# Rebuilding the attention of layer 1: two sets of head buffers, exponentials by pairs of heads, normalisation of three batches by DMA, products on GpSimd, and a new order on every engine

## The reference

```python
x = x + _L1_attn_ref(_L1_cond_ref(x, side, side, L1_cond_w, L1_cond_u, cond), ..., Wqkv, Wproj, bproj)
# attention: 16 heads of 16, no mask
attn = softmax(einsum('gqd,gkd->gqk', q, k) / sqrt(16));  ctx = einsum('gqk,gkd->gqd', attn, v)
out = ctx @ Wproj.T + bproj
# a gate: a, b decay by `decay` at each token, forward and backward
ek = exp(min(k, 30)); ekv = ek * v;  nf, df = scan(ekv, ek);  nb, db = reverse scan(ekv, ek)
euk = exp(min(u + k, 30))
num = nf + nb - ekv + euk * v;  den = df + db - ek + euk
out = sigmoid(r) * (num / max(den, 1e-8)) * (0.8 + 0.2 * tf)
```

## Time and profile before

| | |
|---|---|
| median of 3 runs | 1052.66 us (1048.91 to 1054.09) |
| span of the profiled execution | 1051.6 us |
| PE busy | 919.1 us (87%) |
| DVE busy | 787.0 us (75%) |
| ACT busy | 522.8 us (50%) |
| POOL busy | 248.1 us (24%) |
| attention of layer 1 | about 413 to 595 us of the span |

### The profile page before, as it was taken

How to read it: one execution, slowest core, us unless ns; L and a number is a source line. 1 busy time by engine, 2 the same in 40 slices (tenths; PEclk the granted TensorE clock), 3 DMA queues, 4 the chain that set the end, 5 groups by cost and what they waited for, 6 DMA issues and landing times.

```text
span 1051.6 us, 14776 instructions
## 1 busy us (share of the span) xinstructions
PE 919.1 (87%) x5524; PEld 674.8 (64%) x5524; DVE 787.0 (75%) x1188; ACT 522.8 (50%) x781; POOL 248.1 (24%) x288
## 2 busy tenths in 40 slices
PE   2899896999999998798888989995868886999998
PEld 1566665777777886555555868862446664778886
DVE  7898883559999895778767689888849897554444
ACT  6354455345545544356366444436747667243332
POOL 5122213023334241000020022301513224012221
PEclk9999998999999999899889999998889999899999
DMA  6000000243434331000000233224010000133331
GB/s 248 1 2 2 1 1 1 100 133 96 145 111 146 113 115 38 1 1 1 1 1 1 71 120 117 91 77 104 1 60 1 1 1 2 30 112 109 117 106 60
DMA packets 28518, 64.07 MB, mean 61 GB/s; under 512 B 10240, under 2 KB 12032, under 8 KB 27680
## 3 DMA queue, kind: packets, MB, share of 16 engines
q1 hardware_dynamic: 28448, 63.14, 18.5%
HBM read 60.37 MB, written 2.76 MB: 60 GB/s over the span
## 4 chain that ended last, share of the span: by engine, by line
PE 58%; DVE 21%; ACT 11%; issue 7%; POOL 1%; DMA 1%; DVEq 0%; SPq 0%; ACTq 0%; POOLq 0%
PE bank L1749 11%; PE bank L1750 10%; PE bank L1751 10%; PE bank L647 4%; PE bank L673 3%; ACT probs L794 2%; DVE act_lo L2098 2%; PE bank L756 2%; DVE wkv_y L192 2%; DVE bank L2093 1%; PE bank L705 1%; DVE bank L2084 1%; PE bank L2327 1%; DVE wkv_y L269 1%; DVE act_s L920 1%
## 5 line engine op out<-in xcount | busy, mean ns | idle before, releaser
L1749 PE MATMUL bank<-h_hi,w_gu_hi 128*128 128x512 f32 x416 | 168.1, 404 | 14.9 <-DVE act_lo L2098 9.9
L1896 ACT ACTIVATE act_s<-bank 128x512 f32<-128x512 f32 x104 | 62.0, 597 | 222.0 <-PE bank L1751 222.0
L1750 PE MATMUL bank<-h_hi,w_gu_lo 128*128 128x512 f32 x416 | 165.7, 398 | 0.0
L1751 PE MATMUL bank<-h_lo,w_gu_hi 128*128 128x512 f32 x416 | 165.5, 398 | 0.0
L2084 DVE TENSOR_TENSOR bank<-bank,c_rows 128x512 f32<-128x512 f32 x94 | 65.1, 692 | 87.9 <-PE bank L1751 87.9
L2015 POOL TENSOR_TENSOR w_d_lo<-w_raw,w_d_hi 128x256 fp32r<-128x256 f32 x52 | 46.8, 900 | 266.7 <-ACT w_d_hi L1890 266.7
L1749 PEld LDWEIGHTS bank<-h_hi,w_gu_hi 128*128 128x128 f32 x416 | 78.8, 189 | 40.8 <-issue 18.6
L794 ACT ACTIVATE probs<-bank 128x1536 f32<-128x1536 f32 (+1 forms) x32 | 53.0, 1657 | 95.8 <-PE bank L705 87.6
L1751 PEld LDWEIGHTS bank<-h_lo,w_gu_hi 128*128 128x128 f32 x416 | 79.0, 190 | 19.5
L2010 POOL TENSOR_TENSOR w_gu_lo<-w_raw,w_gu_hi 128x512 fp32r<-128x512 f32 x52 | 71.6, 1377 | 80.1 <-ACT w_gu_hi L1885 80.1
L1750 PEld LDWEIGHTS bank<-h_hi,w_gu_lo 128*128 128x128 f32 x416 | 79.0, 190 | 17.3
(11 more groups left out here) (346 smaller groups left out, 1813.3 us busy)
## 6 DMA issues: line engine op xcount, KB each, us to landing
w_raw<-in_L_w SPq DMA_DIRECT2D x52, 384.0 KB, 3.1
c_rows<-c_L SPq DMA_DIRECT2D x26, 512.0 KB, 3.7
c_rows<-c_L SPq DMA_DIRECT2D x6, 448.0 KB, 3.7
w_attn<-in_L_w_attn SPq DMA_DIRECT2D x2, 1280.0 KB, 7.6
c_rows<-c_L SPq DMA_DIRECT2D x6, 384.0 KB, 3.5
c_rows<-c_L SPq DMA_DIRECT2D x6, 320.0 KB, 3.5
c_rows<-c_L SPq DMA_DIRECT2D x6, 256.0 KB, 3.9
lora_chunks<-w_raw SPq DMA_DIRECT2D x4, 384.0 KB, 2.6
```

Of the source, the lines that this page charges most:

```text
L1749: pe.matmul(o, w_hi, r_hi, start=start, stop=False)
L1750: pe.matmul(o, w_lo, r_hi, start=False, stop=False)
L1751: return pe.matmul(o, w_hi, r_lo, start=False, stop=stop)
L1896: act.activation(act_s[:, half, :], bank[2 * half][:, :], ACT.Silu).then_inc(self.silu, 1)
```

## The change

- **Buffers.** Queries and keys, and the values, get a second set (`heads_2`, `values_2`), which lie over buffers of the experts that are idle in this stage; batches alternate. The maxima get space for all four groups. Scores alternate between banks 0, 1 and banks 2, 3, so step p waits for the maxima of step p-2.
- **Exponentials by pairs.** The transposed scores use banks 4 and 5 only, two heads at a time: `scores_t_pe(b, g, i)` with 4 matmuls in two row groups, then `exp_act(b, g, i)` on 128 x 1024, then the other pair.
- **Normalisation by DMA.** For batches 0 to 2, `sums_pe`, `inv_dve`, `spread_pe` and `norm_dve` are gone. SP writes the four rows of sums to DRAM, reads them back as 128 x 32, DVE takes the reciprocals of that tile, SP writes them to DRAM and broadcasts them to 128 x 1024, and GpSimd multiplies `work[:, b]`. Batch 3 is normalised as before.
- **Gate units.** GpSimd makes the product of the exponential with the side input (two instructions), the sum, and the product with the reciprocal; DVE keeps `den`, one Newton step and the last product.
- **Transposes** of the maxima are ordinary matmuls against an identity, both operands in tiles of the type float32r.
- **Order.** All four functions are written anew; projections of batch b+1 stand between the steps of batch b. The splits of the first weights of `F1` move from the end of batch 2 to the end of batch 3 on ACT, and behind all gate work on GpSimd.

```diff
+heads_2 = under("heads_2", [P, 2 * GROUPS, T])
+values_2 = under("values_2", [P, 2, N])
+sums_2 = under("sums_2", [P, 2, 512])
+sums_dram = nc.dram_tensor("head_sums", (B - 1, 4, N), F32).ap()
+inv_dram = nc.dram_tensor("head_inverses", (B - 1, 4, N), F32).ap()
...
+def pooled_den_dve(dve, o):
+    dve.wait_ge(wkv_exp, o + 1)
+    dve.wait_ge(wkv_bwd, 2 * o + 2)
+    dve.scalar_tensor_tensor(out=wkv_y[:, :, 1, :], in0=wkv_e[:, :, :], scalar=E30, in1=wkv_y[:, :, 1, :],
+                             op0=ALU.min, op1=ALU.add).then_inc(wkv_den, 1)
+def newton_dve(dve, o):
+    den = wkv_y[:, :, 1, :]
+    dve.wait_ge(wkv_ln, 2 * by_ln(o))
+    dve.scalar_tensor_tensor(out=den, in0=den, scalar=1e-8, in1=wkv_e[:, :, :], op0=ALU.add, op1=ALU.mult).then_inc(wkv_inv, 1)
+def pooled_out_dve(dve, o):
+    n, b = UNITS[o]
+    dve.wait_ge(wkv_inv, inv_at(o) + 2)
+    dve.wait_ge(wkv_summed, pool_steps(o) + 2)
+    dve.scalar_tensor_tensor(out=G[:, G_SLOT[n], :, b * T:b * T + T], in0=wkv_y[:, :, 1, :], scalar=2.0,
+                             in1=wkv_num[:, :, :], op0=ALU.subtract, op1=ALU.mult).then_inc(g_done, 1)
+def ev_pool(pool, o):
+    b = UNITS[o][1]
+    pool.wait_ge(wkv_exp, o + 1)
+    pool.wait_ge(g_done, o)
+    pool.tensor_scalar(wkv_num[:, :, :], wkv_e[:, :, :], E30, -1.0, ALU.min, ALU.mult).then_inc(wkv_ev, 1)
+    pool.wait_ge(wkv_ev, pool_steps(o) + 1)
+    pool.tensor_tensor(wkv_num[:, :, :], wkv_num[:, :, :], side[:, :, b * T:b * T + T], ALU.mult).then_inc(wkv_ev, 1)
+def pooled_sum_pool(pool, o):
+    pool.wait_ge(wkv_ev, pool_steps(o) + 2)
+    pool.wait_ge(wkv_bwd, 2 * o + 2)
+    pool.tensor_tensor(wkv_num[:, :, :], wkv_num[:, :, :], wkv_y[:, :, 0, :], ALU.subtract).then_inc(wkv_summed, 1)
+def product_pool(pool, o):
+    pool.wait_ge(wkv_ln, 2 * by_ln(o))
+    pool.wait_ge(wkv_summed, pool_steps(o) + 1)
+    pool.tensor_tensor(wkv_num[:, :, :], wkv_num[:, :, :], wkv_e[:, :, :], ALU.mult).then_inc(wkv_summed, 1)
...
+    self.qk = (qk, heads_2)
+    self.v = (v_sb, values_2[:, 0, :].rearrange("p (t c) -> p t c", t=2))
+    self.inverse = (values_2[:, 1, :], act_s[:, :, :].rearrange("p a t -> p (a t)"))
+    self.maxes = act_hi[:, :, :].rearrange("p a (g h c) -> p (a g) h c", g=2, h=2)
+    self.ident = act_lo[:, 0, 0:P]
+    self.sums = sums_2[:, 1, 0:32]
+    self.inverses = sums_2[:, 1, 32:64]
+    self.tanh = prob_mem[:, 2 * N:4 * N].rearrange("p (k t) -> p k t", k=KC)
...
+def score_banks(self, p):
+    return 2 * (p % 2)
+def scores_pe(self, pe, b, p):
+    f, m = self.first + b, self.qk[b % 2]
+    if p in (0, 4):
+        pe.wait_ge(n_copied, 4 * f + p // 2 + 2)
+    if b or p >= 2:
+        pe.wait_ge(n_maxed, 8 * f + p - 1)
...
+def scores_t_pe(self, pe, b, g, i):
+    m = self.qk[b % 2]
+    pe.wait_ge(n_added, 4 * (self.first + b) + g + 1)
+    if b or g or i:
+        pe.wait_ge(n_exp, self.half_group(b, g, i) - 1)
+    for k, q0, at in self.keys:
+        for j in (2 * i, 2 * i + 1):
+            rows = slice(SLOT * j, SLOT * j + SLOT)
+            mm = pe.matmul(bank[4 + j % 2][:, at:at + T], m[rows, GROUPS + g, k * P:k * P + P],
+                           m[rows, g, 0:T], start=True, stop=True, tile_position=(SLOT * j, 0))
+    mm.then_inc(n_scores_t, 1)
...
+    if sources[-1] < B - 1:
+        pe.wait_ge(n_scaled, sources[-1] + 1)
+    if sources[0] == 0:
+        if tb == 0:
+            pe.wait_ge(n_maxed, 8 * (self.first + B))
+        if tb == 2:
+            pe.wait_ge(n_exp, self.half_group(B - 1, 3, 1))
...
 def pe(self, pe):
     pe.wait_ge(attn_w[self.name], 32)
+    for b in range(-1, B + 1):
+        self.scores_t_pe(pe, b, 0, 0)
+        self.mix_pe(pe, b - 1, 3)
+        self.scores_pe(pe, b, 5)
         self.turn_pe(pe, b, 1)
         self.scores_pe(pe, b, 6)
+        self.scores_t_pe(pe, b, 0, 1)
+        self.proj_pe(pe, b + 1, 0)
+        self.scores_t_pe(pe, b, 1, 0)
         self.mix_pe(pe, b, 0)
         self.turn_pe(pe, b, 2)
         self.scores_pe(pe, b, 7)
+        self.scores_t_pe(pe, b, 1, 1)
+        self.proj_pe(pe, b + 1, 1)
+        self.scores_t_pe(pe, b, 2, 0)
+        self.mix_pe(pe, b, 1)
         self.turn_pe(pe, b, 3)
+        self.scores_t_pe(pe, b, 2, 1)
+        self.scores_pe(pe, b + 1, 0)
+        self.proj_pe(pe, b + 1, 2)
+        self.scores_pe(pe, b + 1, 1)
+        self.scores_t_pe(pe, b, 3, 0)
+        self.proj_pe(pe, b + 1, 3)
+        self.scores_pe(pe, b + 1, 2)
+        self.scores_t_pe(pe, b, 3, 1)
+        self.mix_pe(pe, b, 2)
+        if b == B - 1:
+            self.out_pe(pe, 0, range(B - 2))
+        self.turn_pe(pe, b + 1, 0)
+        self.scores_pe(pe, b + 1, 3)
+        self.scores_pe(pe, b + 1, 4)
+        self.values_pe(pe, b + 1)
+    self.out_pe(pe, 1, range(B - 2))
     self.sums_pe(pe, B - 1)
+    self.out_pe(pe, 0, (2,))
+    self.out_pe(pe, 1, (2,))
     self.spread_pe(pe, B - 1, 0)
     self.spread_pe(pe, B - 1, 1)
     self.out_pe(pe, 0, (B - 1,))
...
     self.out_pe(pe, 2, range(B))
     self.out_pe(pe, 3, range(B))
...
+def exp_act(self, act, b, g, i):
+    at = self.half_group(b, g, i)
+    act.wait_ge(n_scores_t, at)
+    if b or g >= 2:
+        act.wait_ge(n_mixed, 4 * (self.first + b) + g - 1)
+    elif g == 1:
+        act.wait_ge(n_gated, self.first + B)
+    act.activation(self.p_t[g % 2][:, 2 * i:2 * i + 2, :], banks[:, 4:6, :], ACT.Exp).then_inc(n_exp, 1)
...
 def act(self, act):
     self.tanh_act(act)
+    for b in range(-1, B + 1):
+        self.exp_act(act, b - 1, 3, 0)
         self.heads_act(act, b, 3)
+        self.relu_act(act, b, 0)
+        self.ln_act(act, b, 0)
+        self.row_act(act, b, 1)
+        self.exp_act(act, b - 1, 3, 1)
+        self.exp_act(act, b, 0, 0)
+        self.ctx_act(act, b - 1, 1)
         self.scale_act(act, b, 1, 0)
+        self.scale_act(act, b, 1, 1)
+        self.exp_act(act, b, 0, 1)
+        self.units_exp_act(act, b, 1)
+        self.heads_act(act, b + 1, 0)
+        self.exp_act(act, b, 1, 0)
+        self.relu_act(act, b, 1)
+        self.ln_act(act, b, 1)
+        self.exp_act(act, b, 1, 1)
+        self.row_act(act, b + 1, 0)
+        self.heads_act(act, b + 1, 1)
+        self.exp_act(act, b, 2, 0)
         self.ctx_act(act, b, 0)
+        self.scale_act(act, b + 1, 0, 0)
+        self.exp_act(act, b, 2, 1)
+        self.scale_act(act, b + 1, 0, 1)
+        self.heads_act(act, b + 1, 2)
+        self.units_exp_act(act, b + 1, 0)
+        if b == B - 1:
             for p in (0, 1):
                 F1.split_gu_act(act, p)
                 F1.split_d_act(act, p)
...
+def inverse_dve(self, dve, b):
+    dve.wait_ge(n_norm_in, 160 * b + 80)
+    dve.reciprocal(self.inverses, self.sums).then_inc(n_inv, 1)
 def dve(self, dve):
+    for b in range(1, B):
+        self.gate_dve(dve, b)
+    for b in range(B + 1):
+        self.inverse_dve(dve, b - 2)
+        self.newton_dve(dve, b - 1, 1)
+        self.max_dve(dve, b - 1, 7)
+        self.made_dve(dve, b - 1, 1)
+        self.scan_dve(dve, b, 0, False, 0)
+        self.add_dve(dve, b - 1, 3)
+        self.scan_dve(dve, b, 0, False, 1)
+        self.scan_dve(dve, b, 0, True, 0)
+        self.scan_dve(dve, b, 0, True, 1)
         self.max_dve(dve, b, 0)
+        self.den_dve(dve, b, 0)
         self.max_dve(dve, b, 1)
         self.max_dve(dve, b, 2)
         self.add_dve(dve, b, 0)
+        self.newton_dve(dve, b, 0)
         self.max_dve(dve, b, 3)
+        self.max_dve(dve, b, 4)
+        self.made_dve(dve, b, 0)
         self.values_dve(dve, b)
+        self.scan_dve(dve, b, 1, False, 0)
+        self.scan_dve(dve, b, 1, False, 1)
         self.add_dve(dve, b, 1)
+        self.scan_dve(dve, b, 1, True, 0)
+        self.scan_dve(dve, b, 1, True, 1)
         self.max_dve(dve, b, 5)
+        self.den_dve(dve, b, 1)
         self.max_dve(dve, b, 6)
         self.add_dve(dve, b, 2)
...
+def scaled_pool(self, pool, b):
+    pool.wait_ge(n_norm_in, 160 * b + 160)
+    m = work[:, b, :]
+    pool.tensor_tensor(m, m, self.inverse[b % 2], ALU.mult).then_inc(n_scaled, 1)
...
+def pool(self, pool):
+    ones = self.v[1]
+    ends = sum_rows[:, :, :].rearrange("p g c -> p (g c)")
+    pool.wait_ge(self.x_ready, self.x_value)
+    pool.tensor_tensor(act_hi[:, 0, :], ends, ends, ALU.subtract).then_inc(n_zeroed, 1)
+    pool.wait_ge(self.x_ready, self.x_value + 2)
+    pool.tensor_tensor(act_hi[:, 1, :], ends, ends, ALU.subtract).then_inc(n_zeroed, 1)
+    pool.tensor_copy(self.ident, ident[:, :]).then_inc(n_zeroed, 1)
+    pool.memset(ones, 0.0).then_inc(n_zeroed, 1)
+    pool.wait_ge(n_zeroed, 5)
+    pool.memset(ones[:, :, 16::SLOT], 1.0).then_inc(n_zeroed, 1)
+    for b in range(B + 1):
+        self.ev_pool(pool, b, 0)
+        self.sum_pool(pool, b, 0)
+        self.product_pool(pool, b, 0)
+        self.scaled_pool(pool, b - 2)
+        self.ev_pool(pool, b, 1)
+        self.sum_pool(pool, b, 1)
+        self.product_pool(pool, b, 1)
+    for p in (0, 1):
+        F1.gu_pool(pool, p)
+        F1.d_pool(pool, p)
```

(81 more changed lines are left out.)

285 lines of the change are left out of this document (169 added, 116 removed).

## The result

The changed kernel takes 1021.70 us (median of 4 runs, 1018.82 to 1033.05) against 1050.79 us of the kernel before (4 runs, 1046.45 to 1054.09). The ratio is 0.9752, with a 95% interval of 0.9713 to 0.9792: 2.5% faster. The forecast was 1026.8 in a range of 1013 to 1042. The profiled execution took 1021.96 us, its span is 1020.2, and the mean granted clock 0.960.

What follows compares the result with a forecast made beforehand. Layer 1's attention was taken as bound by a loop of hand-offs, 41.15 us per batch, and by PE after the change. Time = 927.8 + 3P + L, with period P = 32 and clock loss L = 3: 1026.8 us, range 1013 to 1042.

Steps and rivals of the forecast that it cites:

- first exponential: Start of layer 1's attention: gates and scans fill DVE's early gap, first exponential at 432.4 instead of 436.8.
- three periods: Layer 1's attention, batches 0 to 2: each takes P = 32 us instead of 41.15.
- last batch to sums, with L: Batch 3, first exponential to sums: 21.2 us by the walk, plus 3 us lost to lower clock over the stage.
- sums to the end of the span: Everything behind batch 3's sums: as before, from 578.5 to 1051.6 in the old profile, 473.1 us.
- The period: Steady batches: double buffers let projections fill PE, which becomes the bound at 30.3 us; 1.7 added, P = 32.
- the meetings: Steady batches: five neighbouring PE steps in different row groups overlap, saving 0.55 us each, bounds 0 and 1.1.
- what a walk misses: Steady batches: 1.7 us added to the walked period of 30.3, for things like GpSimd's contention.
- The end of the stage: Last batch: projections fall away, DVE and ACT keep their latency; sums 21.2 us after its first exponential.
- L = 3: Layer 1's attention: matmul time lost to lower clock is 3 us, from layer 0's 0.02 of 140 us.
- rival of the clock: Layer 1's attention: clock stays as it is (L = 15, P = 32) or the pipeline slips: 1038.8 us; chance 0.22.
- rival of a filled PE: Layer 1's attention: PE filled without gaps, P = 30.3 and L = 0: 1018.7 us; chance 0.18.
- the chain of DMAs: Normalisation of batch 2: both parts of its stores and loads are hidden, with 2.5 and 3.6 us to spare.

Runs made afterwards that it cites:

- the added load: Changed kernel with two dummy projections added in each of batches 0 to 2: 1034.85 us, ratio 0.9872 to the kernel before.
- the run with fewer meetings: Changed kernel with the halves of each transposed score group exchanged, so two neighbouring steps per batch overlap in different row groups instead of five: 1024.45 us.
- real filling: Changed kernel with output projection of finished sources moved into the last batch, plus one dummy projection: 1011.73 us, ratio 0.9656 to the kernel before.

## Why the prediction was right, and where it was not

The sum, term by term, in the profiled execution:

| term | forecast | measured |
|---|---|---|
| first exponential | 432.4 | 429.19, of which 3.2 by a stage that began earlier |
| three periods | 3 x 32 = 96 | 83.8 |
| last batch to sums, with L | 21.2 + 3 | 36.5 |
| sums to the end of the span | 473.1 | 470.7 |
| own time over span | 1.1 | 1.8 |
| sum | 1026.8 | 1022.0 |

- **The period.** The mechanism was right: the double banks break the loop of hand-offs and PE becomes the bound (shown by one pair of banks, and by the added load). The size was off by 4 us. PE's work in a batch is 26.84 us (the period without a gap) and not 30.3. Of these 3.5 us, 1.2 are the meetings, five at 0.80 us instead of 0.55 (shown by the run with fewer meetings). The rest is mostly steps and mixes priced at 1.1 us each, which take 0.95 to 1.07 when one stands right behind the other. The 1.7 us added for what a walk misses was needed in part: the three periods are 3.3 us longer than three without a gap, mostly by PE's gaps in the first and third and the clock of 0.94 in the first.
- **The end of the stage.** This step failed. It priced the last batch by latencies at full clock and put L = 3 for the whole stage, by likeness to layer 0. The batch took 36.5 us against 21.2 by the walk. Of these 15.3 us the clock has at least 9.6 (26.9 with real filling, though PE does more there). By an estimate from the records it has about 11, since a half takes 2.08 us instead of 1.13, a mix 1.94 instead of 1.07, and so on from 518.93 to 546.68. The other 4 or so are hand-offs that the walk left out. So the clock's share was mis-sized threefold or more.
- **Why the clock fell here** is only in part shown. Without projections PE stands idle 2.4 us once and 1.2 us three times, waiting for exponentials, since halves and exponentials take turns on the one pair of banks 4 and 5. Work in these holes keeps the clock up (shown). The forecast counted the missing projections as time saved. But a last batch without projections isn't enough by itself, as the kernel before shows, with its 22.2 us at a clock of 1.00: it made four heads' scores at once into four banks, and had the spreads of batch 2 among its steps. Which of these made the difference is open: a changed kernel with four heads at once in its last batch was not run. Likeness to layer 0 couldn't give the size either. The stretch behind L = 3 ends at 165, and layer 0's last batch goes on to its sums at 177; its clock falls too, but only within 10 us:

```profile
160.00:165.00 5.00, 5.00 (x33) 3.89 (x32) 1.72 (x3) 1.31 (x2) 0.00 (x0) 0.63 0.00 0
165.00:170.00 5.00, 5.00 (x26) 3.71 (x29) 0.38 (x1) 2.25 (x5) 1.22 (x2) 0.69 0.00 0
```

- **The total was right by luck.** The rival of the clock was near on L and wrong on the period, the rival of a filled PE the other way round, and 12 us of error in one term stand against 12 us in the other. The 5 us that are left come from a stage that began earlier and a shorter rest, which the forecast didn't have.
- **The rule of the Trainium skill** ("TensorE: Matmul & The Clock Gate", A second HAM failure mode) says that frequent micro-idles between groups of matmuls that cycle through PSUM banks let the clock swing between its levels. The trace agrees in part: in the last batch, with gaps of 2.41 and then 1.2 us, the clock fell, but it stayed at the lower level for 28 us and didn't swing. In the second and third batch, with no gap and with one of 1.07 us, it was 1.00.
- **VectorE and GpSimd.** VectorE was forecast at 24.6 us per batch plus up to 2.8 for contention, and has 25.8 to 26.8 in the two steady batches. GpSimd has 13.6 to 14.4 instead of 12.6: its tensor_scalar L302 takes 1.99 us and its last product L316 1.56, where 1.27 was assumed for each.
- **The start, the chain of DMAs, the experts' weights** held: the first exponential is where it was forecast once the 3.2 us of the stage before are taken off; the inverses land in time; the experts begin 16.1 us after the sums (16.7 before), with split weights ready. Of the 2.4 us that the rest behind the sums is shorter, this is 0.6; the others lie in later stages and weren't followed.
- A single buffer for heads was not tried: the new order would wait for itself. The transposes as ordinary matmuls were not run by themselves either; a turn takes PE 0.41 to 0.44 us before and after.

## What to carry to other kernels

When a pipeline is tightened, look at its last round by itself: what is prepared for the next round falls away there, and in the new rhythm that work was what kept TensorE full. Moving real work into the holes (an output projection of finished sources) was worth more than the one reordering of that round that was tried, 10 us against 3, though hardly more than dummy work in them (8 us). And a forecast's terms should be checked one by one even where the total is right.

## What the runs showed of the hardware

- Two steps of 32-row matmuls in different row groups took 1.12 us together, two in the same row groups 1.92, one by itself 1.13.
- The 128x512 tensor_scalar with two operations on GpSimd took 1.99 us in the mean (1.92 in seven of eight), the tensor_tensor of the same size 1.27.
- Beside GpSimd's 128x1024 product a VectorE product went from 0.69 to 1.80 us (484.43, with the product from 483.33 on); scans, in places where GpSimd was idle, stayed at 1.21.
- In a batch mostly of short matmuls of 32 rows or columns, with a gap of 2.41 us and then three of 1.2, the clock stayed at 1.2 GHz for 28 us, in which PE was busy 24.4. With the gap of 2.41 cut to 1.28 it fell all the same; with matmuls of 128 rows and columns in the gaps it stayed at 2.4 GHz.
- The same two gaps of 1.35 and 1.07 us in the first batch left the clock at 1.00, 0.94 or, in one stretch, 0.63, in three kernels with the same instructions there.
